# Second products of two expert layers as three fp16 terms, with a tile's block addresses asked for together

## The reference

```
x = x + 0.5 * L0_ffn(layernorm(x))    # 24 experts, hidden 512, top 2
x = x + L0_attn(layernorm(x))         # linear attention, 16 heads
x = x + 0.5 * L0_ffn(layernorm(x))
x = x + 0.5 * L1_ffn(layernorm(x))    # 8 experts, hidden 256, top 2, and a shared one
x = x + L1_attn(layernorm(x))         # causal attention with rotary positions
x = x + 0.5 * L1_ffn(layernorm(x))
```

```
h = gelu(x @ w1[e] + b1[e])           # exact gelu
y = h @ w2[e] + b2[e]                 # "the second product"
out += share[token, e] * y
```

## Time and profile before

| | |
|---|---|
| median of 3 runs | 1033.47 us (1031.43 to 1034.35) |
| the profiled execution | 1034.46 us |
| its span | 1033.1 us |
| granted TensorE clock, mean | 0.952 |
| TensorE busy, matmul / weight load | 903.7 us (87%) / 786.1 us |
| VectorE busy | 563.8 us (55%) |
| ScalarE busy | 476.0 us (46%) |
| GpSimd busy | 493.5 us (48%) |
| HBM read, written | 40.13 MB, 56.90 MB |

### The profile page before, as it was taken

One profiled execution on the slowest core, in us unless ns is written; L12 is line 12 of the kernel. 1 busy time (PEld: TensorE's weight loads), 2 busy tenths in 40 slices (PEclk: granted clock), 3 DMA queues, 4 the chain that ended last, 5 costly groups with the idle time before them and its releaser, 6 DMA issues.

```text
span 1033.1 us, 25972 instructions
## 1 busy us (share of the span) xinstructions
PE 903.7 (87%) x8524; PEld 786.1 (76%) x8524; DVE 563.8 (55%) x2208; ACT 476.0 (46%) x804; POOL 493.5 (48%) x519
## 2 busy tenths in 40 slices
PE   4478999998999599999899999996999999999860
PEld 2237999986899577899898898983778878778850
DVE  6785800055787065785038500588793988874022
ACT  3224454348654358645345444452538354454320
POOL 0551047073015771007474561776744447477765
PEclk9768999999999899999999999998999999999995
DMA  9946764452352543363452356832633143436772
GB/s 317 385 148 175 214 142 104 96 116 47 63 113 81 121 83 76 54 173 101 114 121 65 90 125 137 164 83 66 112 103 100 53 100 88 100 97 157 159 162 74
DMA packets 219623, 126.02 MB, mean 122 GB/s; under 512 B 137456, under 2 KB 199792, under 8 KB 219248
## 3 DMA queue, kind: packets, MB, share of 16 engines
q1 hardware_dynamic: 203120, 90.77, 37.2%
...
HBM read 40.13 MB, written 56.90 MB: 94 GB/s over the span
## 4 chain that ended last, share of the span: by engine, by line
PE 57%; DVE 16%; POOL 9%; DMA 7%; issue 7%; ACT 4%; SPq 0%; POOLq 0%; ACTq 0%; DVEq 0%
PE bank L1530 21%; PE bank L1506 6%; PE bank L1508 5%; PE bank L1507 5%; POOL rows L2214 5%; POOL got L2234 4%; PE bank L1392 3%; DMA got<-y_l,slot_index 3%; PE bank L1345 2%; DMA turned<-rows 2%; PE bank L1528 2%; PE bank L1321 2%; PE bank L1364 2%; DVE x_res L2030 2%; PE bank L1402 2%
## 5 line engine op out<-in xcount | busy, mean ns | idle before, releaser
L1530 PE MATMUL bank<-blocks_l,hid 128*128 x2496 | 361.5, 287 | 0.0
L2214 POOL DMA_INDIRECT rows<-rows_sent,slot_index x192 | 186.3, 970 | 325.5 <-issue 248.3
L2234 POOL DMA_INDIRECT got<-y_l,slot_index x256 | 243.8, 953 | 188.9 <-PE bank L1530 74.5
L1530 PEld LDWEIGHTS bank<-blocks_l,hid 128*128 128x128 f32 x2496 | 312.1, 192 | 6.3 <-issue 1.3
L1678 ACT ACTIVATE hid<-bank 128x512 f32<-128x512 f32 (+1 forms) x316 | 185.2, 592 | 262.0 <-PE bank L1508 255.4
L1506 PE MATMUL bank<-turned,blocks_l 128*128 128x128 f16 x1248 | 238.9, 224 | 41.5 <-DMA turned<-rows 25.6
L2030 DVE SCALAR_TENSOR_TENSOR x_res<-got,share,x_res 128x128 f32<-128x128 f32 x256 | 78.2, 348 | 321.8 <-DMA got<-y_l,slot_index 319.4
L1508 PE MATMUL bank<-turned,blocks_l 128*128 128x128 f16 x1248 | 238.8, 224 | 0.0
L1507 PE MATMUL bank<-turned,blocks_l 128*128 128x128 f16 x1248 | 237.5, 223 | 0.0
L1506 PEld LDWEIGHTS bank<-turned,blocks_l 128*128 x1248 | 125.7, 101 | 56.2 <-issue 51.5
L1507 PEld LDWEIGHTS bank<-turned,blocks_l 128*128 x1248 | 124.6, 100 | 4.1 <-issue 1.3
...
## 6 DMA issues: line engine op xcount, KB each, us to landing
...
got<-y_l,slot_index POOLq DMA_INDIRECT x256
...
```

The source lines that it names most:

```text
L1530: m = t.do.matmul(out, hid[:, j * H + c * P:j * H + c * P + P], second[:, at], start=False, stop=(c == C - 1))
L2214: d = g.do.indirect_dma_start(rows_dram[s], at, rows[:, 2 * D * i:2 * D * i + 2 * D], None)
L2234: d = g.do.indirect_dma_start(got_mem[slot][:, col:col + D], None, y_dram[layer][s][layer.team(ev.i)], at)
```

## The change

Four things are changed. First, each second product is made of three fp16 terms. `hidden` writes gelu back into its own bank, a second ScalarE instruction (`high_hidden`) writes 16 times the value as fp16 into `hid`, and VectorE (`low_hidden`) writes what is left as fp16. W2 is split at the start like W1: ScalarE writes the upper half (`upper_w2`), TensorE makes the rest in a bank (`second_left`: identity by raw, minus the upper half), ScalarE writes the lower half. `layer2` then has, per 128 hidden columns, upper by high, upper by low and, after a wait for the low hidden half, lower by high, and `copy_y` scales back. Second, the weights are one tensor per 128 hidden columns and half (`first_high_l0_0` and so on) and not one block per expert, and a tile's addresses are asked for ahead of its matmuls. Third, the placement of the norms of the rounds after the first goes from VectorE (four instructions) to ScalarE (four) with one short VectorE instruction. Fourth, the planner's costs, its table and some details follow: parking is eight transfers, W1's pieces are cut by 128 columns, the `l1` bank is held until the low half is made.

```diff
-        "l1": [[(PE, 0.68, 0.22), (SC, 0.58, 0.16)]], "l2": [[(PE, 1.03 if unit == 1 else 1.17, 0.22)]], "ystore": [[(SC, 0.55, 0.15)] + copied(256)],
+        "l1": [[(PE, 0.7 if unit == 1 else 0.76, 0.22), (SC, 0.58, 0.16)]], "hid": [[(SC, 0.6, 0.16), (VE, 0.7, 0.1)]],
+        "l2": [[(PE, (0.75 if layer.terms else 1.03) if unit == 1 else (0.8 if layer.terms else 1.17), 0.22)]], "ystore": [[(SC, 0.55, 0.15)] + copied(256)],
...
+                c, q = divmod(ev.i, layer.parts)
+                for i, at in enumerate(spans(PART_EXPERTS)):
+                    e = q * PART_EXPERTS + i
                     t.do.matmul(bk[:, at], ccol("ident"), raw[:, at], start=True, stop=False)
-                    m = t.do.matmul(bk[0:LAST, at], spread(hcol("select_cut")[:, e:e + 1], LAST), last, start=False, stop=True)
+                    m = t.do.matmul(bk[0:LAST, at], spread(hcol("select_cut")[:, e:e + 1], LAST), last[:, P * c:P * c + P], start=False, stop=True)
                 m.then_inc(w1_part.sem, 1)
+
+            def second_left(ev, layer):
+
+                raw, loaded = raw_of(load_of(ev))
+                bk = bank_of(ev)
+                t.wait_ge(const_loaded, 16)
+                t.wait_ge(half_loaded, 32)
+                t.wait_ge(*loaded.after(load_of(ev)))
+                bank_free(ev)
+                t.do.matmul(bk[:, :], ccol("ident"), raw, start=True, stop=False)
+                t.wait_ge(*w2_high.after(Ev("upper" + ev.kind[5:], *ev[1:])))
+                m = t.do.matmul(bk[:, :], minus, part_of(seconds[layer][0], layer, ev), start=False, stop=True)
+                m.then_inc(w2_left.sem, 1)
...
-            def block_for(ev, j):
-
-                layer = LAYER[ev.p]
-                return blocks[layer][:, bass.ds(place[ev.s, ev.p][ev.i * layer.unit + j], layer.block)]
+            def expert_of(ev, j):
+                return place[ev.s, ev.p][ev.i * LAYER[ev.p].unit + j]
+
+            def cut_of(mem, e):
+
+                return mem[:, :].rearrange("p (e h) -> p e h", h=P)[:, bass.ds(e, 1), :].rearrange("p e h -> p (e h)")
+
+            def address(e, name, size, columns, last):
+                nc.lower_val(e * columns * size + (sb_at[name] + last * size), [TENSOR])
+
+            def first_addresses(layer, e):
+
+                for c in range(layer.chunks):
+                    for half in ("high", "low"):
+                        address(e, f"first_{half}_{layer.name}_{c}", 2, P, P - 1)
+
+            def second_addresses(layer, e):
+
+                nc.lower_val(e * 2 + sb_at[f"select_{layer.name}"], [TENSOR])
+                for c in range(layer.chunks):
+                    if layer.terms:
+                        for half in ("high", "low"):
+                            address(e, f"second_{half}_{layer.name}_{c}", 2, P, 0)
+                    else:
+                        address(e, f"second_{layer.name}_{c}", 4, P, 0)
...
-                    high, low, _, _ = block_parts(block_for(ev, j), H)
-                    for c, at in enumerate(spans(C)):
+                    e, (high, low) = expert_of(ev, j), firsts[layer]
+                    first_addresses(layer, e)
+                    for c in range(C):
                         out = hb[:, j * H + c * P:j * H + c * P + P]
-                        t.do.matmul(out, high[:, at], xh, start=True, stop=False)
-                        t.do.matmul(out, high[:, at], xl, start=False, stop=False)
-                        m = t.do.matmul(out, low[:, at], xh, start=False, stop=True)
+                        t.do.matmul(out, cut_of(high[c], e), xh, start=True, stop=False)
+                        t.do.matmul(out, cut_of(high[c], e), xl, start=False, stop=False)
+                        m = t.do.matmul(out, cut_of(low[c], e), xh, start=False, stop=True)
...
-                t.wait_ge(*hidden_gelu[ev.s].after(l1))
+                    t.wait_ge(block_back, 16 * len(pieces[L1]))
+                if layer.terms:
+                    t.wait_ge(*hidden_high[ev.s].after(Ev("hid", *ev[1:])))
+                else:
+                    t.wait_ge(*hidden_gelu[ev.s].after(l1))
...
-                    _, _, second, select = block_parts(block_for(ev, j), H)
-                    t.do.matmul(out, spread(select), bcol("b2_0" if layer is L0 else "b2_1"), start=True, stop=False)
-                    for c, at in enumerate(spans(C)):
-                        m = t.do.matmul(out, hid[:, j * H + c * P:j * H + c * P + P], second[:, at], start=False, stop=(c == C - 1))
+                    e = expert_of(ev, j)
+                    second_addresses(layer, e)
+                    t.do.matmul(out, spread(select[layer][:, bass.ds(e, 1)]), bcol("b2_0" if layer is L0 else "b2_1"), start=True, stop=False)
+                    if not layer.terms:
+                        for c in range(C):
+                            m = t.do.matmul(out, hid[:, j * H + c * P:j * H + c * P + P], cut_of(seconds[layer][0][c], e), start=False, stop=(c == C - 1))
+                        continue
+                    (high, low), terms = seconds[layer], hid.bitcast(F16)
+                    for c in range(C):
+                        upper = terms[:, j * H + c * P:j * H + c * P + P]
+                        t.do.matmul(out, upper, cut_of(high[c], e), start=False, stop=False)
+                        t.do.matmul(out, upper, cut_of(low[c], e), start=False, stop=False)
+                    t.wait_ge(*hidden_low[ev.s].after(Ev("hid", *ev[1:])))
+                    for c in range(C):
+                        lower = terms[:, SEQ + j * H + c * P:SEQ + j * H + c * P + P]
+                        m = t.do.matmul(out, lower, cut_of(high[c], e), start=False, stop=(c == C - 1))
...
+            def place_norm(ev):
+                sm, xn, x = norm_mem[plan.norms.at[ev]], xn_mem[plan.xn.at[ev]], x_res[ev.s]
+                a.wait_ge(*norm_done[ev.s].after(ev))
+                old = plan.xn.before[ev]
+                for read in xn_read(old) if old else ():
+                    a.wait_ge(*read)
+                for i in range(BT):
+                    root, minus_mean = sm[:, 2 * BT + i:2 * BT + i + 1], sm[:, 3 * BT + i:3 * BT + i + 1]
+                    m = a.do.activation(xn[:, D * i:D * i + D], x[:, BT * ev.i + i, :], ACT.Identity, bias=minus_mean, scale=root)
+                m.then_inc(norm_placed[ev.s].sem, 1)
...
+            def upper_w2(ev, layer):
+                raw, loaded = raw_of(load_of(ev))
+                a.wait_ge(*loaded.after(load_of(ev)))
+                a.do.activation(part_of(seconds[layer][0], layer, ev), raw, ACT.Copy, scale=W_SCALE).then_inc(w2_high.sem, 1)
+
+            def lower_w2(ev, layer):
+                a.wait_ge(*w2_left.after(ev))
+                a.do.activation(part_of(seconds[layer][1], layer, ev), bank_of(ev)[:, :], ACT.Copy, scale=W_SCALE).then_inc(w2_low.sem, 1)
...
+            def hid_free(l1):
+
+                old = plan.hid.before[l1]
                 if old:
                     a.wait_ge(*expert_out[old.s].after(Ev("l2", *old[1:])))
-                m = a.do.activation(hid_mem[plan.hid.at[ev]][:, 0:n], bank_of(ev)[:, 0:n], ACT.Gelu, scale=1 / (X_SCALE * W_SCALE))
-                m.then_inc(hidden_gelu[ev.s].sem, 1)
+                else:
+                    a.wait_ge(*w1_low.after_all(w1_splits[0]))
+                    second_ready(a, L0)
+
+            def hidden(ev):
+                layer = LAYER[ev.p]
+                n = layer.filled(ev.i) * layer.H
+                hb = bank_of(ev)[:, 0:n]
+                a.wait_ge(*hidden_made[ev.s].after(ev))
+                if not layer.terms:
+                    hid_free(ev)
+                out = hb if layer.terms else hid_mem[plan.hid.at[ev]][:, 0:n]
+                a.do.activation(out, hb, ACT.Gelu, scale=1 / (X_SCALE * W_SCALE)).then_inc(hidden_gelu[ev.s].sem, 1)
+
+            def high_hidden(ev):
+                l1, n = Ev("l1", *ev[1:]), LAYER[ev.p].filled(ev.i) * LAYER[ev.p].H
+                hid = hid_mem[plan.hid.at[l1]].bitcast(F16)
+                a.wait_ge(*hidden_gelu[ev.s].after(l1))
+                hid_free(l1)
+                m = a.do.activation(hid[:, 0:n], bank_of(l1)[:, 0:n], ACT.Copy, scale=HID_SCALE)
+                m.then_inc(hidden_high[ev.s].sem, 1)
...
-                a.do.activation(y_mem[plan.y.at[ev]][:, 0:n], ob[:, 0:n], ACT.Copy).then_inc(y_copied[ev.s].sem, 1)
+                a.do.activation(y_mem[plan.y.at[ev]][:, 0:n], ob[:, 0:n], ACT.Copy, scale=1 / OUT_SCALE if layer.terms else 1.0).then_inc(y_copied[ev.s].sem, 1)
...
+            def low_hidden(ev):
+                l1, n = Ev("l1", *ev[1:]), LAYER[ev.p].filled(ev.i) * LAYER[ev.p].H
+                hid = hid_mem[plan.hid.at[l1]].bitcast(F16)
+                v.wait_ge(*hidden_high[ev.s].after(ev))
+                m = v.do.scalar_tensor_tensor(hid[:, SEQ:SEQ + n], bank_of(l1)[:, 0:n], HID_SCALE, hid[:, 0:n], ALU.mult, ALU.subtract)
+                m.then_inc(hidden_low[ev.s].sem, 1)
...
```

(4 more changed lines are left out.)

265 lines of the change are left out of this document (164 added, 101 removed).

## The result

The kernel after takes 1042.01 us (median, 1040.42 to 1043.06), the kernel before in the same comparison 1032.45 (1031.26 to 1034.35). The ratio is 1.0086, with a 95% interval of 1.0067 to 1.0104: 0.9% slower, where 994 us had been forecast.

What follows compares the result with a forecast made beforehand. TensorE was taken to bound the kernel in the early expert rounds, not the last stretch. The terms, -60 + 3 + 10 + 7 = -40 us, took 1034.46 to 994.5, stated as 994 us; range 960 to 1034.

Steps and rivals of the forecast that it cites:

- The second products: Expert second products on TensorE: an L0 tile falls from 1.72 to 1.44 us, an L1 unit from 1.89 to 1.54.
- Rival A: TensorE's fp16 stream does not hold its pace, 0.083 us per product: 1120 us, half way 1080; chance 0.07.
- What of it counts: Tile gains on TensorE, credited full, half or none by how full each stretch was: 60 us gained.
- their 13 us: Forecast costs of the two hidden halves: 3 us for ScalarE's pace and 10 us for holds on VectorE.
- ScalarE's pace: ScalarE's gelu, fp16 copy and share of y copy, 1.35 us per tile against TensorE's 1.44: costs 3 us (0 to 30).
- Rival C: ScalarE becomes the bound, at 1.6 us a tile: 1025 us; chance 0.13.
- Holds on VectorE: Low halves wait in VectorE's order behind gather adds: 24 groups at 0.4 us each, 10 us (0 to 72).
- Rival B: Holds on VectorE at the gather adds, 3 us a group: 72 us instead of 10, so 1056; chance 0.10.
- The split at the start: Splitting W2 before the first expert tile, partly in TensorE's idle time: costs 7 us (0 to 28).
- Norms, 0: Later rounds' norm placements move from VectorE to ScalarE: -5 to +5 us, taken as 0.
- The signs of being wrong: Tile above 1.6 us, TensorE waiting over 30 us for low halves, or the split's end moving by 20 us.
- The range and the chances: 960 to 1034 us at 8 in 10; faster 0.78, same 0.06, slower 0.16; the forecast itself 0.62.

Runs made afterwards that it cites:

- sets A to C: Three of five comparison sets, each on one chip beside the kernel before, which took 1189 to 1202 us there, 15 to 16% more.
- new table: Planner costs set to the trace, some 12,000 table changes tried: kernel after 1153.74, 1148.98, 1158.27 us; kernel before, done alike, 1154.86, 1171.86 us.

## Why the prediction was wrong

- **The second products.** Right, and a little better: 1.39 us per L0 tile, forecast 1.44. Rival A, and the rule of about 81 ns that the Trainium skill gives (TensorE: Matmul & The Clock Gate, section "Back-to-back issue gap"), fall: in the trace 25 products and four address instructions take 1.39 us, 0.056 a product.
- **What of it counts.** This is the step that failed. I took the stretches of the kernel before as they stood, and gave full credit where TensorE was full, half where it was mixed: 60 us. That holds only if the other engines' orders stay as good as they were. The diff replaced the whole table, the order excerpts showed it, and I priced the moved places (holds, the start) and put the order as a whole at nothing, without a reason. Measured: with both halves gone the kernel is level with the kernel before (1032.55 us), where the forecast without their 13 us and with 7 for the split would be 981; some 50 us are missing. The instructions of the kernel without low halves in another order take 53 us less (1033.12 to 980.08), and in that order the product, with its split of W2, is worth 63 us. So 60 us was about the size of the gain, in an order that suits the terms; the order of the diff did not give it. How the loss divides between an order that is worse for any product and one in which TensorE's time does not bind is known from sets A to C alone: the float32 product in this order is 1.9 to 2.2% above the kernel before, and the terms gave back 0.5%.
- **The clock, not in the sum.** The chain from waits to clock was left out: the mean granted clock fell to 0.916, and some 76 us more of the span lie at 1.2 GHz, where a first product takes 0.105 us and not 0.056 (24 of them from 847.93 to 850.46 us, 12 from 858.97 us). It comes with the waits, at 331 to 391 us above all, and no run here separates its share of the loss.
- **ScalarE's pace, 3 us.** Right: taking the copy away as well gave 0.6 us. Rival C falls.
- **Holds on VectorE, 10 us.** The size was right (8 to 9 us for all that the low halves cost), and the hold at 853 us shows the mechanism, though TensorE waited only 1.47 us in it. Rival B, at 2.1 us a group or more, falls.
- **The split at the start, 7 us.** The first tile did come 10.7 us late, but that the split alone had to be paid for was wrong: without its lower half the tile still came 10.2 us late, as the rows were no earlier. Split and rows ended together, and no run took both away.
- **Norms, 0.** The placements were mis-sized (65.8 us on ScalarE, forecast 46), but the sign of the move was right: undone, it costs 10 to 11 us more in this order.
- **The signs of being wrong.** None of the three came: the tile takes 1.39 us (limit 1.6), TensorE waits 19.0 us for low halves (30), and the end of the splits moved from 81.5 to 99.0 us (20). All three watched the priced terms, and none the order.
- **The range and the chances.** None of the rivals was "the new order is worse than the old one". A table of 46 numbers, nearly all of them new, moves every engine, and deserved a rival of its own on the slow side.

What stays open: which places of the order make up the loss (one scatter moved made it 2% worse, the routing moved changed nothing that shows); what the float32 product takes in the order of the kernel after, and each kernel with its new table, where the kernel before takes 1032 us; and so what the change is worth there when both orders are equally good; and what sets A, B and C have in common.

The complete version that beats both is the kernel after with the new table: 0.960 to 0.967 of the kernel before in sets A, B and C.
